# A GCN layer with gated residual and layer norm on one core: the last i-group in three runs of 256, 128 and 128 columns, and another order of the last tiles' small operations

## The chip, the cores and the metric

The program runs on one core of a Trainium2 chip. The metric is device time in microseconds (us). Of the kernel before there are three timed runs, with a median of 396.89 us, and one profiled execution.

## The reference, cut to what matters

There are 4096 nodes with two feature sets of width 128, x and spatial_x, and a dense 4096 x 4096 matrix adj. All is float32.

```python
def _gcn_layer(x, adj, W, b):
    d_inv_sqrt = (jnp.sum(adj, axis=1) + 1e-09) ** (-0.5)
    msg = d_inv_sqrt[:, None] * adj * d_inv_sqrt[None, :] @ x
    return jax.nn.relu(msg @ W + b)
H_f = _gcn_layer(feature_x, adj, W_f, b_f)
H_s = _gcn_layer(spatial_x, adj, W_s, b_s)
attn = jax.nn.sigmoid(jnp.concatenate([H_f, H_s], axis=1) @ W_att + b_att)
x = _layernorm(x + attn * H_f + (1.0 - attn) * H_s, axis=-1)
```

## The kernel before, in words

Nodes are cut into T = 32 tiles of P = 128 and G = 8 i-groups of IB = 512 columns, an i-group being four output tiles (GT). The big product is sums[feature, i] = sum over j of Y[j, feature] * A^T[j, i], where Y is the two feature sets side by side (256 wide), each row scaled by D = degree^-0.5. TensorE does it in blocks (e, t): run e has an i-group, a list of j-tiles t to accumulate over, a PSUM pair and a column range. For each of the two feature halves a block is three matmuls (lines 380 to 382), since each operand is split into a high and a low float32r part: Yh x Ah, Yl x Ah, Yh x Al. Each matmul has its own 128x128 weights (a half of Yh or Yl), and the moving operand is Ah or Al. `plan` lists the runs and groups their blocks into K = 64 items, each one transfer of 1 MB of A^T; ScalarE makes Ah (line 657), VectorE makes Al (line 471). `sweeps(k)` orders an item's blocks: run by run, all tiles of half 0 and then all of half 1. As a run's half ends, VectorE adds it from PSUM to acc (`evacuate_half`, line 493).

In the last 16 items each i-group gets its last eight j-tiles. The last i-group (tiles 28 to 31) is two runs of 256 columns, each one item of eight blocks: tiles 28 and 29, then 30 and 31.

When an i-group is complete, each of its tiles r goes through this chain, over four engines:

- TensorE: product with W_f and W_s (`weigh`, `weigh_half`; line 390, plain float32). `weigh_half` waits for the evacuation of one half, does both tiles, then waits for the other half.
- VectorE: `affine` (line 507, scale and bias into z), `logit` (line 516, max(z,0) times W_att with its sum).
- ScalarE: `relu` (line 688), `gate` (line 693, sigmoid).
- `mix` on GpSimd (lines 803 and 804) or, for the tiles in OWN_MIX, on VectorE (lines 523 and 524): H_f - H_s, and x + H_s.
- VectorE: `join` (line 537), x + H_s + attn * (H_f - H_s) with its row sum.
- GpSimd: `mean` (line 809). ScalarE: `square` (line 697). GpSimd: `deviation` (lines 814, 817 and 822; the power -0.5 and the shift). ScalarE: `normalise` (line 702).
- SP: the store of the tile (line 366), in the order of tiles 0 to 27 and then BY_VECTOR = 30, 28, 29, 31.

The last four tiles differ: VectorE normalises them (`normalise_last`, lines 561 and 565), and tiles 30 and 31 get their statistics on VectorE (`join_last`, lines 546 to 555) and their power on GpSimd (`last_deviation`, line 827). Nothing is scheduled at run time: each engine's order is the order of the code, and inside the item loop `group_at` places a group's steps so many items after its run's end. All that comes after the loop, on each engine, is written out by hand, and that is what the change edits.

Of the kernel before, what the change touches and what calls it, by code (L numbers as in the profile page):

```python
# [24 lines left out]
def plan(T):  # L25
# [43 lines left out]
    order += [(G - 1, s6 + s7), (G, s6 + s7)]  # L69
    items.extend([(first + g, t) for t in s] for g, s in order)  # L70
    return runs, items


def build(nc, At, adj, xs_in, W_f, W_s, b_f, b_s, W_att, b_att, out):
# [11 lines left out]
    FIRST_LAST = len(runs) - G - 1  # L86
# [108 lines left out]
    with ExitStack() as ctx:  # L195
# [175 lines left out]
        def _(pe):  # L371
# [62 lines left out]
            for k in range(K):  # L434
# [25 lines left out]
            weigh_half(HALVES[1])  # L460
# [3 lines left out]
        def _(dve):  # L464
# [76 lines left out]
            def join_last(r):  # L541

                n = r - (T - 2)
# [3 lines left out]
                                         in1=xs[:, r, 0:F], op0=ALU.mult, op1=ALU.add).then_inc(y_ok, 1)  # L547
                dve.wait_ge(y_ok, r + 1)
# [102 lines left out]
        def _(act):  # L651
# [81 lines left out]
            for r in of_group(TAIL - 3):  # L733
                normalise(r)
# [158 lines left out]
```

## Time and profile before

| | us |
|---|---|
| median of 3 runs (396.66 to 397.29) | 396.89 |
| profiled execution, its own time | 398.95 |
| its span, first to last instruction | 397.1 |
| TensorE busy (matmuls) | 373.2 |
| VectorE busy | 296.6 |
| ScalarE busy | 284.6 |
| GpSimd busy | 145.4 |

The profile is of one execution. PE is TensorE's matmuls and PEld its weight loads, DVE is VectorE, ACT is ScalarE, POOL is GpSimd, SP issues the DMAs. Matmuls are pipelined: one of 128x512 is shown as 0.39 us long, but the next starts 0.23 us after it, so what a matmul costs is read from starts, not from lengths.

### The profile page before, as it was taken

The numbers are of one execution on the slowest core, as the hardware profiler recorded it, in microseconds if no ns is written. First come the engines' busy times: TensorE is split into PE (matmuls) and PEld (weight loads), VectorE is DVE, ScalarE is ACT, GpSimd is POOL, SyncE is SP. The second block draws the span as 40 slices with busy tenths as digits, with TensorE's granted clock in tenths as the row PEclk, the third lists the DMA queues.
The fourth block names the chain that finished last, engine by engine and source line by source line (L and its number), as shares of the span: only waits on it lengthen the run. The fifth ranks groups of instructions, "written<-read, shape, count | busy, mean of one in ns | idle before, by whom it ended". The sixth has DMA issues, their size and how long they took to land. (4 is left out here: it accounts for less than half of the span.)

```text
span 397.1 us, 5306 instructions
## 1 busy us (share of the span) xinstructions
PE 373.2 (94%) x1748; PEld 310.7 (78%) x1748; DVE 296.6 (75%) x417; ACT 284.6 (72%) x346; POOL 145.4 (37%) x189
## 2 busy tenths in 40 slices
PE   2997999999999999999999999999889999999991
PEld 2785786878888888888888888888668888888991
DVE  2768984968668793969397775919857797888896
ACT  3777788788878887777878887858492656578565
POOL 1000002571177226730459100002010417877765
PEclk9999999999999999999999999999999999999997
DMA  8999999999999999999999999999946534344011
GB/s 302 415 424 419 419 422 420 420 423 420 422 419 419 420 421 418 363 404 427 421 418 421 416 390 421 414 411 413 360 177 262 210 106 171 149 168 150 19 38 53
DMA packets 25371, 132.86 MB, mean 335 GB/s; under 512 B 2944, under 2 KB 7936, under 8 KB 11008
## 3 DMA queue, kind: packets, MB, share of 16 engines
q1 hardware_dynamic: 25344, 132.53, 82.7%
q8 instruction: 14, 0.23, 0.2%
q14 instruction: 13, 0.11, 0.1%
HBM read 130.42 MB, written 2.10 MB: 334 GB/s over the span
## 5 line engine op out<-in xcount | busy, mean ns | idle before, releaser
L380 PE MATMUL sums<-Ah,Yh 128*128 128x512 f32 (+1 forms) x528 | 204.0, 386 | 7.4 <-DVE Yl L482 4.1
L382 PE MATMUL sums<-Al,Yh 128*128 128x512 f32 (+1 forms) x528 | 202.2, 383 | 0.0
L381 PE MATMUL sums<-Ah,Yl 128*128 128x512 f32 (+1 forms) x528 | 202.2, 383 | 0.0
L471 DVE TENSOR_TENSOR Al<-raw,Ah 128x2048 fp32r<-128x2048 f32 (+1 forms) x70 | 153.6, 2201 | 35.3 <-ACT Ah L657 32.8
L657 ACT ACTIVATE Ah<-raw 128x2048 fp32r<-128x2048 f32 (+1 forms) x70 | 123.2, 1768 | 46.1 <-DMA raw<-in_At 32.3
L670 ACT ACTIVATE nat<-nat 128x2048 f32<-128x2048 f32 x54 | 103.6, 1918 | 28.4 <-DMA nat<-in_adj 27.2
L380 PEld LDWEIGHTS sums<-Ah,Yh 128*128 128x128 f32 x528 | 99.2, 188 | 30.4 <-DVE Yl L482 7.0
L382 PEld LDWEIGHTS sums<-Al,Yh 128*128 128x128 f32 x528 | 99.2, 188 | 19.6
L381 PEld LDWEIGHTS sums<-Ah,Yl 128*128 128x128 f32 x528 | 99.2, 188 | 18.9
L493 DVE TENSOR_TENSOR acc<-sums,acc 128x512 f32<-128x512 f32 (+1 forms) x122 | 77.5, 676 | 45.6 <-PE sums L382 45.6
L797 POOL TENSOR_TENSOR S<-S,raw 128x512 f32<-128x512 f32 x32 | 56.4, 1761 | 24.6 <-DMA raw<-in_At 21.8
L762 POOL TENSOR_SCALAR dg<-rs 128x1 f32<-128x1 f32 x23 | 13.8, 598 | 128.4 <-ACT nat L670 128.2
L697 ACT ACTIVATE fin<-xs,less 128x128 f32<-128x128 f32 x30 | 11.7, 390 | 18.6 <-POOL less L809 18.6
L803 POOL TENSOR_TENSOR fin<-fin 128x128 f32<-128x128 f32 x29 | 13.9, 480 | 21.8 <-ACT fin L688 21.8
L804 POOL TENSOR_TENSOR xs<-xs,fin 128x128 f32<-128x128 f32 x29 | 20.7, 713 | 0.0
L482 DVE SCALAR_TENSOR_TENSOR Yl<-xs,D,Yh 128x256 fp32r<-128x256 f32 x32 | 20.0, 641 | 0.0
L537 DVE SCALAR_TENSOR_TENSOR xs<-fin,att,xs 128x128 f32<-128x128 f32 x30 | 12.3, 423 | 8.6 <-POOL xs L804 8.5
L390 PE MATMUL sums<-Wfs,acc 128*128 128x128 f32 x128 | 16.3, 277 | 0.1
L390 PEld LDWEIGHTS sums<-Wfs,acc 128*128 128x128 f32 x128 | 15.6, 191 | 1.0 <-DVE acc L493 0.3
L681 ACT ACTIVATE Yh<-xs,D 128x256 fp32r<-128x256 f32 x32 | 15.2, 494 | 1.4 <-POOL D L789 0.9
L783 POOL TENSOR_TENSOR dsum<-rs 128x4 f32<-128x4 f32 x2 | 1.9, 975 | 37.8 <-ACT nat L670 19.5
L688 ACT ACTIVATE fin<-nat 128x256 f32<-128x256 f32 x32 | 11.5, 408 | 5.9 <-DVE nat L507 5.8
(49 smaller groups left out, 139.0 us busy)
## 6 DMA issues: line engine op xcount, KB each, us to landing
raw<-in_At SPq DMA_DIRECT2D x64, 1024.0 KB, 9.3
nat<-in_adj SPq DMA_DIRECT2D x48, 1024.0 KB, 11.4
nat<-in_adj SPq DMA_DIRECT2D x8, 768.0 KB, 12.5
xs<-in_xs SPq DMA_DIRECT2D x7, 512.0 KB, 11.3
nat<-in_adj SPq DMA_DIRECT2D x8, 256.0 KB, 9.2
out<-xs SPq DMA_DIRECT2D x32, 64.0 KB, 1.9
xs<-in_xs SPq DMA_DIRECT2D x2, 128.0 KB, 6.8
xs<-in_xs SPq DMA_DIRECT2D x1, 256.0 KB, 11.6
```

What stands on the lines that cost most here:

```text
L380: pe.matmul(to, Yh[:, t % YRING, hs], high, start=first, stop=False)
L381: pe.matmul(to, Yl[:, t % YRING, hs], high, start=False, stop=False)
L382: mm = pe.matmul(to, Yh[:, t % YRING, hs], low, start=False, stop=last)
L390: return pe.matmul(sums[:, 3, bank, c + half * H:c + (half + 1) * H], acc[:, r // GT, half, q * P:(q + 1) * P], Wfs[:, half * H:(half + 1) ...
L471: dve.tensor_tensor(Al[:, k % SPLITS, a * IB:b * IB], raw[:, k % RAWS, a * IB:b * IB], Ah[:, k % SPLITS, a * IB:b * IB], ALU.subtract).the ...
L482: dve.scalar_tensor_tensor(out=Yl[:, r % YRING, :], in0=xs[:, r, :], scalar=D[:, r:r + 1], in1=Yh[:, r % YRING, :].bitcast(F32), op0=ALU.mult,
L493: dve.tensor_tensor(acc[:, g, half, a:b], sums[:, pair, half, 0:b - a], acc[:, g, half, a:b], ALU.add).then_inc(evac_ok, 1)
L657: act.activation(Ah[:, k % SPLITS, a * IB:b * IB], raw[:, k % RAWS, a * IB:b * IB], ACT.Copy).then_inc(high_ok, b - a)
L670: act.activation(nat[:, n % NATS, :], nat[:, n % NATS, :], ACT.Copy, accum_out=rs[:, r, h:h + 1]).then_inc(rs_act, 1)
L681: act.activation(Yh[:, r % YRING, :], xs[:, r, :], ACT.Copy, scale=D[:, r:r + 1]).then_inc(Yh_ok, 1)
L797: pool.tensor_tensor(S[:, g, :], S[:, g, :], raw[:, k % RAWS, j * IB:(j + 1) * IB], ALU.add).then_inc(block_sum_ok, 1)
L804: pool.tensor_tensor(xs[:, r, 0:F], xs[:, r, 0:F], f[:, H_S], ALU.add).then_inc(res_ok, 1)
```

## The change

The second run of the last i-group is cut in two: its 256 columns become one run of 128 columns for tile 30 and one for tile 31, both in the last item, of 16 blocks now. The third run has PSUM pair 1.

```diff
-    runs.append((G - 1, s6 + s7, 2, (0, IB // 2)))
-    runs.append((G - 1, s6 + s7, 0, (IB // 2, IB)))
+    runs.append((G - 1, s6 + s7, 2, (0, 2 * P)))
+    runs.append((G - 1, s6 + s7, 0, (2 * P, 3 * P)))
+    runs.append((G - 1, s6 + s7, 1, (3 * P, IB)))
...
+    items.append([(first + G - 1, t) for t in s6 + s7])
+    items.append([(first + e, t) for e in (G, G + 1) for t in s6 + s7])
...
-    HALVES = [range(LAST, LAST + 2), range(LAST + 2, T)]
-    OWN_MIX = [LAST - 2, LAST - 1, T - 2]
+    LAST_ROWS = [range(LAST, LAST + 2), range(T - 2, T - 1), range(T - 1, T)]
+    PAIR = LAST_ROWS[0]
+    OWN_MIX = [T - 1]
...
-                    if k == K - 1 and step == GT:
-                        weigh_half(HALVES[0])
+                    if k == K - 1 and step == 2 * GT:
+                        weigh_last(0)
+                    if k == K - 1 and step == 6 * GT:
+                        weigh_last(1)
...
-            weigh_half(HALVES[1])
+            weigh_last(2)
```

`weigh_last(n)` is `weigh_half` for the rows of LAST_ROWS[n]: tiles 28 and 29 are weighed after half 0 of the second run, tile 30 after half 0 of the third, tile 31 at the end. On VectorE `join_last` is cut in two: it ends with the join, and `spread_last` does the statistics. The order behind the item loop:

```diff
-            for r in of_group(TAIL - 2):
+            for r, q in zip(of_group(TAIL - 2), of_group(TAIL - 1)):
                 join(r)
+                affine(q)
             evacuate_half(FIRST_LAST + TAIL, 0)
-            for r in of_group(TAIL - 1):
-                affine(r)
             for r in of_group(TAIL - 1):
                 logit(r)
             evacuate_half(FIRST_LAST + TAIL, 1)
-            mix(LAST - 2)
-            mix(LAST - 1)
+            join(LAST - 4)
+            for r in PAIR:
+                affine(r)
+            join(LAST - 3)
             join(LAST - 2)
             join(LAST - 1)
-            join(LAST - 4)
-            for r in HALVES[0]:
-                affine(r)
-            join(LAST - 3)
-            for r in HALVES[0]:
-                logit(r)
             evacuate_half(FIRST_LAST + TAIL + 1, 0)
             evacuate_half(FIRST_LAST + TAIL + 1, 1)
-            for r in HALVES[0]:
-                join(r)
-            for r in HALVES[1]:
-                affine(r)
+            for r in PAIR:
                 logit(r)
-            mix(T - 2)
+            affine(T - 2)
+            logit(T - 2)
+            evacuate_half(FIRST_LAST + TAIL + 2, 0)
+            join(PAIR[0])
+            evacuate_half(FIRST_LAST + TAIL + 2, 1)
+            join(PAIR[1])
             join_last(T - 2)
+            affine(T - 1)
+            logit(T - 1)
+            spread_last(T - 2)
+            mix(T - 1)
             join_last(T - 1)
+            spread_last(T - 1)
```

On ScalarE the relus of group 6 (tiles 24 to 27) come ahead of the squares of group 5, and of group 6 only tile 24 is squared before the gates of tiles 28 to 30; tiles 25 to 27 are squared between gate 30 and relu 31. On GpSimd:

```diff
-            mix(HALVES[0][0])
+            mix(LAST - 4)
+            mean(of_group(TAIL - 2))
+            for r in range(LAST - 3, LAST):
+                mix(r)
+            deviation(of_group(TAIL - 2))
+            mix(PAIR[0])
             mean(of_group(TAIL - 1))
-            mix(HALVES[0][1])
-            mean(HALVES[0])
+            mix(PAIR[1])
+            mix(T - 2)
+            mean(PAIR)
             deviation(of_group(TAIL - 1))
-            mix(T - 1)
             last_deviation([T - 2])
-            deviation(HALVES[0])
+            deviation(PAIR)
             last_deviation([T - 1])
```

What this makes of the engines' orders, at three places.

TensorE in the last item. Before, where tiles 28 and 29 are weighed (L390), amid half 0 of the second run:

```order
L380 MATMUL sums<-Ah,Yh 128x256
L381 MATMUL sums<-Ah,Yl 128x256
L382 MATMUL sums<-Al,Yh 128x256
L390 MATMUL sums<-Wfs,acc 128x128 x4
L380 MATMUL sums<-Ah,Yh 128x256
```

And with the change, where tile 30 is weighed (L393), between the halves of the third run:

```order
L383 MATMUL sums<-Ah,Yh 128x128
L384 MATMUL sums<-Ah,Yl 128x128
L385 MATMUL sums<-Al,Yh 128x128
L393 MATMUL sums<-Wfs,acc 128x128 x2
L383 MATMUL sums<-Ah,Yh 128x128
```

The three lines of a block stand 16 times in the item before, with 256 columns, and 32 times now, with 128.

VectorE from the last two evacuations (L493) on, before; the first two joins (L537) are those of tiles 28 and 29:

```order
L493 TENSOR_TENSOR acc<-sums,acc 128x256 x2
L537 SCALAR_TENSOR_TENSOR xs,ysum<-fin,att,xs 128x128 x2
L507 SCALAR_TENSOR_TENSOR nat<-sums,D,bias 128x256
L516 SCALAR_TENSOR_TENSOR nat,lg<-nat,watt 128x256
L507 SCALAR_TENSOR_TENSOR nat<-sums,D,bias 128x256
L516 SCALAR_TENSOR_TENSOR nat,lg<-nat,watt 128x256
L523 TENSOR_TENSOR fin<-fin 128x128
L524 TENSOR_TENSOR xs<-xs,fin 128x128
L546 SCALAR_TENSOR_TENSOR xs<-fin,att,xs 128x128
L551 BN_STATS st<-xs 128x6
```

With the change, from the affine of tile 30 (L512) on:

```order
L512 SCALAR_TENSOR_TENSOR nat<-sums,D,bias 128x256
L521 SCALAR_TENSOR_TENSOR nat,lg<-nat,watt 128x256
L498 TENSOR_TENSOR acc<-sums,acc 128x128
L542 SCALAR_TENSOR_TENSOR xs,ysum<-fin,att,xs 128x128
L498 TENSOR_TENSOR acc<-sums,acc 128x128
L542 SCALAR_TENSOR_TENSOR xs,ysum<-fin,att,xs 128x128
L549 SCALAR_TENSOR_TENSOR xs<-fin,att,xs 128x128
L512 SCALAR_TENSOR_TENSOR nat<-sums,D,bias 128x256
L521 SCALAR_TENSOR_TENSOR nat,lg<-nat,watt 128x256
L558 BN_STATS st<-xs 128x6
```

The affine and the logit of tile 30 have moved ahead of the last evacuations, and the join of tile 29 (the second L542) still stands behind the very last one.

GpSimd's end before, from the mix of tile 29 on (L803 and L804):

```order
L803 TENSOR_TENSOR fin<-fin 128x128
L804 TENSOR_TENSOR xs<-xs,fin 128x128
L809 TENSOR_TENSOR less<-ysum,share 128x2
L814 TENSOR_SCALAR vare<-ysq 128x4
L817 TENSOR_TENSOR rstd<-vare,mhalf 128x4
L822 TENSOR_TENSOR shift<-less,rstd 128x4
L803 TENSOR_TENSOR fin<-fin 128x128
```

With the change, from the mix of tile 30 on (L812 and L813):

```order
L812 TENSOR_TENSOR fin<-fin 128x128
L813 TENSOR_TENSOR xs<-xs,fin 128x128
L818 TENSOR_TENSOR less<-ysum,share 128x2
L823 TENSOR_SCALAR vare<-ysq 128x4
L826 TENSOR_TENSOR rstd<-vare,mhalf 128x4
L831 TENSOR_TENSOR shift<-less,rstd 128x4
L836 TENSOR_TENSOR rstd<-vare,mhalf 128x1
```

The mean of tiles 28 and 29 stands ahead of the deviation of tiles 24 to 27 in both; the mix of tile 31 no longer follows.

## Rows read from the trace of the kernel before

**Rows 1.** The page, busy time of each engine

```profile
PE 373.2 (94%) x1748; PEld 310.7 (78%) x1748; DVE 296.6 (75%) x417; ACT 284.6 (72%) x346; POOL 145.4 (37%) x189
```

**Rows 2.** Windows: stretch, busy us (instructions) by engine, clock, DMA share, GB/s

```profile
380.10:387.40 7.30, 7.19 (x59) 6.93 (x58) 7.00 (x31) 5.12 (x18) 5.69 (x12) 1.00 0.14 39
```

**Rows 3.** Timeline of PE, 367 to 388 us: start, length, instruction

```profile
367.84 0.39 PE L380 MATMUL sums<-Ah,Yh 128*128 128x512 f32 x1
...
372.60 0.28 PE L380 MATMUL sums<-Ah,Yh 128*128 128x256 f32 x1
...
375.48 1.95 PE L390 MATMUL sums<-Wfs,acc 128*128 128x128 f32 x16
377.18 0.37 PE L380 MATMUL sums<-Ah,Yh 128*128 128x256 f32 x1
...
380.14 0.28 PE L380 MATMUL sums<-Ah,Yh 128*128 128x256 f32 x1
...
381.58 1.43 PE L390 MATMUL sums<-Wfs,acc 128*128 128x128 f32 x8
382.77 0.37 PE L380 MATMUL sums<-Ah,Yh 128*128 128x256 f32 x1
...
387.05 0.28 PE L382 MATMUL sums<-Al,Yh 128*128 128x256 f32 x1
```

**Rows 4.** L424's matmuls by form (busy, mean ns), and timeline of their loads

```profile
L424 PE MATMUL sums<-ones,S 128*128 128x1 f32 x16 | 1.8, 245 | 0.0
252.81 1.88 PEld L424 LDWEIGHTS sums<-ones,S 128*128 128x128 f32 x16
```

**Rows 5.** Timeline of PEld at 37.9 us, after a wait

```profile
37.88 0.19 PEld L380 LDWEIGHTS sums<-Ah,Yh 128*128 128x128 f32 x1 [0.84 <-DVE Yl L482]
37.99 0.19 PEld L381 LDWEIGHTS sums<-Ah,Yl 128*128 128x128 f32 x1
```

**Rows 6.** Timeline of DVE, 387.3 to 389.4 us

```profile
387.37 0.42 DVE L493 TENSOR_TENSOR acc<-sums,acc 128x256 f32<-128x256 f32 x1 [0.30 <-PE sums L382]
...
388.20 0.35 DVE L537 SCALAR_TENSOR_TENSOR xs<-fin,att,xs 128x128 f32<-128x128 f32 x1
...
388.47 0.48 DVE L507 SCALAR_TENSOR_TENSOR nat<-sums,D,bias 128x256 f32<-128x256 f32 x1
388.99 0.42 DVE L516 SCALAR_TENSOR_TENSOR nat<-nat,watt 128x256 f32<-128x256 f32 x1
```

**Rows 7.** Timeline of POOL, 388.7 to 390.8 us

```profile
388.70 0.20 POOL L809 TENSOR_TENSOR less<-ysum,share 128x2 f32<-128x2 f32 x1 [1.09 <-ACT fin L697]
...
390.42 0.33 POOL L822 TENSOR_TENSOR shift<-less,rstd 128x4 f32<-128x4 f32 x1
```

**Rows 8.** Timeline of ACT, 390.5 to 392.9 us

```profile
390.52 0.39 ACT L697 ACTIVATE fin<-xs,less 128x128 f32<-128x128 f32 x1
...
391.30 1.63 ACT L702 ACTIVATE xs<-xs,shift,rstd 128x128 f32<-128x128 f32 x4
```

**Rows 9.** Timeline of the SP queue: the last eight stores

```profile
391.80 3.67 SPq L366 DMA_DIRECT2D out<-xs  x8
```

**Rows 10.** Timeline of all engines, 390 to 394.7 us, tiles 30 and 31

```profile
390.21 0.29 DVE L523 TENSOR_TENSOR fin<-fin 128x128 f32<-128x128 f32 x1
390.41 0.28 DVE L524 TENSOR_TENSOR xs<-xs,fin 128x128 f32<-128x128 f32 x1
...
392.12 0.64 POOL L827 TENSOR_TENSOR rstd<-vare,mhalf 128x1 f32<-128x1 f32 x1 [0.51 <-DVE vare L555]
...
394.34 0.35 DVE L565 TENSOR_SCALAR xs<-xs,mv,rstd 128x128 f32<-128x128 f32 x1
```

**Rows 11.** Timeline of DVE: a join of group 5, and affines 24 to 27

```profile
376.52 0.42 DVE L537 SCALAR_TENSOR_TENSOR xs<-fin,att,xs 128x128 f32<-128x128 f32 x1 [0.45 <-POOL xs L804]
...
378.88 1.65 DVE L507 SCALAR_TENSOR_TENSOR nat<-sums,D,bias 128x256 f32<-128x256 f32 x4
```

**Rows 12.** Timeline of POOL: the mix of tile 20

```profile
374.62 0.46 POOL L803 TENSOR_TENSOR fin<-fin 128x128 f32<-128x128 f32 x1
375.04 0.46 POOL L804 TENSOR_TENSOR xs<-xs,fin 128x128 f32<-128x128 f32 x1
```

More of the change, by code:

```diff
@@ L65, in plan @@
     runs.extend((g, s6 + s7, (g + 1) % 3, (0, IB)) for g in range(G - 1))
-    runs.append((G - 1, s6 + s7, 2, (0, IB // 2)))
-    runs.append((G - 1, s6 + s7, 0, (IB // 2, IB)))
+    runs.append((G - 1, s6 + s7, 2, (0, 2 * P)))
+    runs.append((G - 1, s6 + s7, 0, (2 * P, 3 * P)))
+    runs.append((G - 1, s6 + s7, 1, (3 * P, IB)))
     order = [(0, s6), (1, s6), (0, s7), (1, s7)] + [(g, s) for g in range(2, G - 1) for s in (s6, s7)]
-    order += [(G - 1, s6 + s7), (G, s6 + s7)]
     items.extend([(first + g, t) for t in s] for g, s in order)
+    items.append([(first + G - 1, t) for t in s6 + s7])
+    items.append([(first + e, t) for e in (G, G + 1) for t in s6 + s7])
     return runs, items
@@ L85, in build @@
     FINAL = K - 2 * G
-    FIRST_LAST = len(runs) - G - 1
+    FIRST_LAST = len(runs) - (G - 1) - 3
     BLK = GT * IB
@@ L175, in build @@
     LAST = (G - 1) * GT
-    HALVES = [range(LAST, LAST + 2), range(LAST + 2, T)]
-    OWN_MIX = [LAST - 2, LAST - 1, T - 2]
-    BY_VECTOR = [T - 2, *HALVES[0], T - 1]
+    LAST_ROWS = [range(LAST, LAST + 2), range(T - 2, T - 1), range(T - 1, T)]
+    PAIR = LAST_ROWS[0]
+    OWN_MIX = [T - 1]
+    BY_VECTOR = [T - 2, *PAIR, T - 1]
     POOL_MIX = [r for r in range(T) if r not in OWN_MIX]
@@ L402, in weigh, with weigh_last @@
                     weigh_tile(r, 1).then_inc(w_ok, 1)
-            def weigh_half(rows):
-                part = HALVES.index(rows)
-                evacuated = 2 * evac_no[FIRST_LAST + TAIL + part]
+            def weigh_last(n):
+                rows = LAST_ROWS[n]
+                evacuated = 2 * evac_no[FIRST_LAST + TAIL + n]
                 pe.wait_ge(z_ok, rows[0])
@@ L541, in join_last @@
             def join_last(r):
-                n = r - (T - 2)
                 dve.wait_ge(gate_ok, r + 1)
@@ L547, in join_last, with spread_last @@
                                          in1=xs[:, r, 0:F], op0=ALU.mult, op1=ALU.add).then_inc(y_ok, 1)
+            def spread_last(r):
+                n = r - (T - 2)
                 dve.wait_ge(y_ok, r + 1)
@@ L557, in normalise_last @@
             def normalise_last(r):
-                if r in HALVES[0]:
-                    dve.wait_ge(rstd_ok, HALVES[0][-1] + 1)
-                    dve.wait_ge(less_ok, HALVES[0][-1] + 1)
+                if r in PAIR:
+                    dve.wait_ge(rstd_ok, PAIR[-1] + 1)
+                    dve.wait_ge(less_ok, PAIR[-1] + 1)
                     dve.tensor_scalar(xs[:, r, 0:F], xs[:, r, 0:F], less[:, r:r + 1], rstd[:, r:r + 1],
@@ L734, in _ @@
                 normalise(r)
+            for r in of_group(TAIL - 1):
+                relu(r)
             for r in of_group(TAIL - 2):
                 square(r)
-            for r in of_group(TAIL - 1):
+            gate(of_group(TAIL - 1))
+            for r in PAIR:
                 relu(r)
-            gate(of_group(TAIL - 1))
             for r in of_group(TAIL - 2):
                 normalise(r)
-            for r in HALVES[0]:
-                relu(r)
             square(LAST - 4)
-            square(LAST - 3)
-            gate(HALVES[0])
-            square(LAST - 2)
-            square(LAST - 1)
-            for r in HALVES[1]:
-                relu(r)
-                gate([r])
-            for r in HALVES[0]:
+            gate(PAIR)
+            relu(T - 2)
+            gate([T - 2])
+            for r in of_group(TAIL - 1)[1:]:
+                square(r)
+            relu(T - 1)
+            gate([T - 1])
+            for r in PAIR:
                 square(r)
@@ L848, in of_group @@
                 return range(g * GT, (g + 1) * GT)
-            for g in range(TAIL):
+            for g in range(TAIL - 1):
                 if g >= 1:
@@ L854, in _ @@
                 for r in of_group(g):
-                    if r not in OWN_MIX:
-                        mix(r)
-            mix(HALVES[0][0])
+                    mix(r)
+            mix(LAST - 4)
+            mean(of_group(TAIL - 2))
+            for r in range(LAST - 3, LAST):
+                mix(r)
+            deviation(of_group(TAIL - 2))
+            mix(PAIR[0])
             mean(of_group(TAIL - 1))
-            mix(HALVES[0][1])
-            mean(HALVES[0])
+            mix(PAIR[1])
+            mix(T - 2)
+            mean(PAIR)
             deviation(of_group(TAIL - 1))
-            mix(T - 1)
             last_deviation([T - 2])
-            deviation(HALVES[0])
+            deviation(PAIR)
             last_deviation([T - 1])
```

## The prediction

> **What bounds the kernel now.** I read the page first: TensorE is busy 94% of the span [rows 1], so the kernel is TensorE's stream of matmuls, and what follows its last product. Its granted clock in the stretch of the last item is 1.00, the 2.4 GHz level [rows 2]. Then I read the timelines of the last 25 us, because the diff touches nothing before 372 us. TensorE's rows show no gap: the first run of the last i-group starts at 372.60, the second at 380.14, and its last accumulating matmul starts at 387.05 and takes 0.28, so sums are complete at 387.33; only one short wait lies in between, before 382.77 [rows 3]. The chain behind that is this. VectorE adds the last half at 387.37, makes joins 28 and 29 (end 388.55) [rows 6]; GpSimd has `mean(28, 29)` and `deviation(24..27)` queued behind join 29, from 388.70 to 390.75 [rows 7]; ScalarE squares tiles 28 and 29 and then normalises 24 to 27 from 391.30, four in 1.63 us and 0.39 apart, so the first ends at 391.77 [rows 8]; the SP queue issues the last eight stores one after another from 391.80 to 395.47 [rows 9], and the span closes at 397.1. Tile 31's own end (norm at 394.34 to 394.69) comes before its place in that queue. So the page's chain, which ends in that last norm, is about 0.4 us short of being the bound: the stores are a queue of eight times 0.46 us, started by the normalisation of tile 24. From the last sum to the first of these stores it is 391.80 - 387.33 = 4.47 us, and 5.3 more to the end of the span.
>
> **What one matmul of 128 columns costs.** This is the term that decides, and no accumulating matmul of that width runs now. In a stream, 24 matmuls of 256 columns take 372.60 to 375.48, 120 ns each; 21 of 512 columns take 367.84 to 372.60, 227 ns each [rows 3]. The 256 more columns cost 107 ns, so columns cost 0.417 ns, and 13 ns are fixed. By that line 128 columns take 53 + 13 = 67 ns. But each matmul here loads its own weights. The 16 passes of L424 multiply only one column each, and still their 16 loads take 1.88 us, the last alone 0.19, so fifteen steps of 112 ns [rows 4]: nothing is left there but the load of 128x128 four-byte weights. That those are plain f32 and ours float32r makes no difference where I can see it: after a stall, when the next load is free to go, L381's load follows L380's by 0.11 us (37.88, 37.99) [rows 5]. A load hides behind 256 columns (107 + 13 > 112), not behind 128. So I take 112 ns; the ends from the nearest rows are 67 ns below (the line through the two widths), 108 ns for the closest reading of the loads, and 120 ns above (the 256-column matmul; half of it can't cost more unless the hardware treats narrow ones in another way, a rival below).
> The Trainium skill (TensorE: Matmul & The Clock Gate, section Back-to-back issue gap) speaks for the change: it gives about 81 ns per matmul of 128 columns in streams of load and matmul, and 56 ns without the load. By 81 ns the time would be 398.1 us as an estimate, by 56 ns 395.7. No row here shows a pitch under 108 ns, and the one-column passes contradict both for four-byte weights.
>
> **The change, part by part.**
> *Last i-group in three runs.* Removed are the 48 matmuls of 256 columns of the second run (48 x 120 ns = 5.8 us), added 96 of 128 columns (96 x 112 ns = 10.75 us). The products with W_f and W_s after 380.14 stay 12 passes until the last sum of the third run starts (8 for tiles 28 and 29, now 4 for tile 30 too; before it was 8): 12 x 112 ns = 1.35 us. Before, the wait at 381.58 to 382.77 held 0.3 us for the evacuation of the first run's second half; it goes, since that is done by 381.7 and now asked for at 382.8. The last sum is complete at 380.14 + 10.75 + 1.35 + 0.17 (the last matmul takes 0.28, not 0.11) = **392.41**, against 387.33: +5.08 us.
> *What follows the last sum.* VectorE adds the last 128 columns (256 take 0.42; with half the columns I let the next operation start after 0.23), then join 29 with 0.35 [rows 6]: 392.45 to 393.03. GpSimd again has `mean(28, 29)` and `deviation(24..27)` queued behind it, the wait that matters: 388.55 to 390.75 is 2.20 us [rows 6, 7], now 393.03 to 395.23. ScalarE has to pass gate 31 and the squares of 28 and 29 first. TensorE's last product needs the evacuation (392.7) and ends about 393.2; affine 31 goes behind joins 29 and 30, 393.4 to 393.9, logit 31 to 394.4 (0.48 and 0.42, 0.52 from the one to the other [rows 6]), gate 31 at 394.45, the squares behind it from 394.65 with 0.39 each [rows 8], so ScalarE is free at 395.43. The normalisation of tile 24 takes 0.48: first store at **395.94**, 3.53 us behind the last sum where it was 4.47. Before, four vector operations for tile 30 and the affine of 31 stood between join 29 and ScalarE's squares; now tile 30 has been sent ahead.
> *Stores.* SP's instructions are unchanged: eight at the same pace, so the end moves with the first, 395.94 - 391.80 = **+4.14 us**. Tile 31 does not take over: from gate 31 at 394.75 with the mix (two of 0.29, 0.20 apart), join, statistics and a power of 0.64 [rows 10] its norm ends near 398.2, about 3.4 us on, and its slot in the queue is at 399.2.
> *Affines laced into joins.* Four joins of group 5 each wait some 0.45 us for a mix on GpSimd [rows 11]; the affines of 24 to 27 (0.39 apart in their stream) now fill those waits, so VectorE is about 1 us earlier at logit 27. That is taken at nothing: VectorE then waits for TensorE, at the next affine already (381.8 to 383.7) and again at 386.6 and 389.7. If TensorE were not late, this 1 us would be the gain.
> *Mixes.* Mixes 26, 27 and 30 go from VectorE (0.40 each) to GpSimd (0.42 for each of two operations [rows 12]), mix 31 the other way. GpSimd idles from about 387.1 to 390.7 in my schedule, waiting for tile 30, so it costs nothing; mix 31 on VectorE stands in the tail of tile 31, covered by the 1.0 us that tile 31 has in hand.
> *Squares, deviations, runs' places in PSUM and the load of the last item* move behind work that is already waiting; that item is as many bytes as before, and the bank of the third run was emptied at 375. Nothing.
>
> **Sum.** +4.1 us. The profiled execution took 398.95 us around its span of 397.1; with the change 403.1. The median of the runs shown, 396.89, is 0.5% under that execution, and the same step on it gives **401.0 us**. With 108 ns a matmul it is 0.4 less, with 120 ns 0.8 more; the tail worked out may be 0.6 off either way: 399.6 to 402.6 for this case.
>
> **Rivals.**
> *The load hides after all.* Float32r weights could be loaded behind the running matmul as long as it streams, so that only 67 ns are left. Then the last sum is complete at 380.14 + 6.43 + 1.35 + 0.22 = 388.14, and with 3.53 us the first store is at 391.67: -0.1 us, 396.8, not slower; it decides from a pitch of 68 ns down, below which the change wins, up to 0.9 us with the scatter of the tail. For it: the fixed 13 ns at both widths show no load at all. Against it: [rows 4, 5].
> *A narrow float32r matmul is run as a plain f32 one.* L390's f32 products of 128 columns appear as two passes each, 16 rows for 8 instructions, 1.70 us from 375.48 to the next matmul at 377.18 and so 106 ns a pass [rows 3], 112 by [rows 4]. If that held for the 96, each would take up to 223 ns: 21.4 us in place of 10.75, so 411.6. For it: only that width and this price stand side by side in the trace. Against it: float32r at 256 and 512 columns is a single pass, and nothing in the instruction but its width changes.
> *The change does what it says and the shorter tail wins.* The tail is 0.94 us shorter in my working; for a gain, TensorE would have to lose less than that, which is the first rival's condition and no case of its own.
>
> **Chances.** 112 ns and its bounds 0.80; hidden loads 0.12; two passes 0.08. Around 396.8, with its scatter, the hidden-load case is 0.04 faster by over 0.2%, 0.05 within 0.2% (0.8 us, about what a measurement can tell here), and 0.03 slower. So faster 0.04, same 0.05, slower 0.91. The predicted time is the likeliest case's. Its own range holds about 0.77; I reach down to 397.6, the slower part of the hidden-load case, and leave the two-pass case out: 397.6 to 402.6.
>
> **What would show it.** Right: matmul rows of 128x128 in the last item 0.11 us apart and their weight loads back to back; the last of them near 392.3; GpSimd's mean of two tiles near 393.2; the first of the last eight stores near 395.9; VectorE with waits of 1 to 2 us for TensorE. Wrong: such rows 0.07 or 0.22 apart, or first store and last sum more than 4.5 or less than 2.5 us apart.

## The result, and the profile after

The changed kernel takes 400.65 us (median of 4 runs, 400.58 to 401.14), the kernel before 397.07 in the runs made beside it: ratio 1.0094, 95% interval 1.0076 to 1.0111. It is slower by 3.6 us. Its profiled execution took 400.63 us around a span of 398.8.

The page of the changed kernel, busy time of each engine, which answers to [rows 1]; its matmuls of 128 columns by form (busy, mean ns | idle before); and a windows row of the narrow stretch with the columns of [rows 2]:

```profile
PE 378.9 (95%) x1796; PEld 316.9 (79%) x1796; DVE 296.3 (74%) x415; ACT 284.6 (71%) x346; POOL 152.7 (38%) x193
```

```profile
L383 PE MATMUL sums<-Ah,Yh 128*128 128x128 f32 x32 | 8.8, 275 | 0.0
```

```profile
377.95:390.30 12.35, 12.35 (x113) 12.34 (x111) 7.70 (x32) 6.65 (x26) 6.93 (x15) 1.00 0.08 23
```

48 more matmuls, TensorE without a gap and its loads busy for 12.34 of 12.35 us, at the 2.4 GHz level. VectorE, busy for 7.00 of 7.30 us in the last stretch before [rows 2], now idles 38% of it. The timeline of PE answers to [rows 3]:

```profile
370.50 0.28 PE L383 MATMUL sums<-Ah,Yh 128*128 128x256 f32 x1
...
378.04 0.22 PE L383 MATMUL sums<-Ah,Yh 128*128 128x128 f32 x1
378.10 0.28 PE L384 MATMUL sums<-Ah,Yl 128*128 128x128 f32 x1
378.21 0.27 PE L385 MATMUL sums<-Al,Yh 128*128 128x128 f32 x1
...
379.44 0.27 PE L384 MATMUL sums<-Ah,Yl 128*128 128x128 f32 x1
...
386.92 0.66 PE L393 MATMUL sums<-Wfs,acc 128*128 128x128 f32 x4
387.34 0.31 PE L383 MATMUL sums<-Ah,Yh 128*128 128x128 f32 x1
...
389.94 0.28 PE L385 MATMUL sums<-Al,Yh 128*128 128x128 f32 x1
390.05 1.03 PE L393 MATMUL sums<-Wfs,acc 128*128 128x128 f32 x4
```

From 378.10 to 379.44 are twelve steps: 112 ns each. The last sum is complete at 389.94 + 0.28 = 390.22 (390.21 unrounded).

The clocks of the two executions can't be compared directly. In this one the first matmul of 256 columns starts at 370.50, in the one before at 372.60 [rows 3], with the same code ahead of it; in the executions below it lies anywhere from 370.4 to 372.5, and in one, two_runs_both, at 377.2. What the stretch after it takes repeats much better. So from here on each kernel is counted from its own first matmul of 256 columns (in four_runs, the first of 128):

| us | before | changed |
|---|---|---|
| first such matmul to the last sum | 14.73 | 19.71 |
| last sum to the first of the last eight stores | 4.47 | 3.37 |
| that store to the end of the span | 5.27 | 5.26 |
| together | 24.47 | 28.34 |

That is +3.87 us, against +3.6 in the medians. The tail behind the last sum, in timelines of DVE, POOL, ACT and SP ([rows 6 to 9]):

```profile
390.25 0.29 DVE L498 TENSOR_TENSOR acc<-sums,acc 128x128 f32<-128x128 f32 x1 [1.00 <-PE sums L385]
390.46 0.34 DVE L542 SCALAR_TENSOR_TENSOR xs<-fin,att,xs 128x128 f32<-128x128 f32 x1
```

```profile
390.95 0.19 POOL L818 TENSOR_TENSOR less<-ysum,share 128x2 f32<-128x2 f32 x1 [1.40 <-DVE xs L542]
...
392.60 0.35 POOL L831 TENSOR_TENSOR shift<-less,rstd 128x4 f32<-128x4 f32 x1
```

```profile
392.69 0.39 ACT L706 ACTIVATE fin<-xs,less 128x128 f32<-128x128 f32 x1
...
393.08 1.63 ACT L711 ACTIVATE xs<-xs,shift,rstd 128x128 f32<-128x128 f32 x4
```

```profile
383.32 13.91 SPq L369 DMA_DIRECT2D out<-xs  x12
```

The chain is the forecast one: join 29, GpSimd's mean and deviation behind it, ScalarE's squares, the normalisation of tile 24, and a queue of eight stores (393.58 to 396.81; the profile prints them with the four of group 5). Where VectorE's time went is in its waits (the number before the arrow): 1.00 us above, and 2.13 us before affine 30:

```profile
387.62 0.48 DVE L512 SCALAR_TENSOR_TENSOR nat<-sums,D,bias 128x256 f32<-128x256 f32 x1 [2.13 <-PE sums L393]
```

### The profile page after: what moved, and what is told of

Its sections match the earlier page's. It is cut to its first block and busy times, and to the rows that moved or that the text cites. A ratio compares the mean times of both kernels' runs of the same rounds, so it can differ in the third digit from the quotient of the medians.

```text
span 398.8 us, 5407 instructions
## 1 busy us (share of the span) xinstructions
PE 378.9 (95%) x1796; PEld 316.9 (79%) x1796; DVE 296.3 (74%) x415; ACT 284.6 (71%) x346; POOL 152.7 (38%) x193
## 5 line engine op out<-in xcount | busy, mean ns | idle before, releaser
L383 PE MATMUL sums<-Ah,Yh 128*128 128x512 f32 (+2 forms) x544 | 208.8, 384 | 3.9 <-DVE Yl L487 2.2
L384 PE MATMUL sums<-Ah,Yl 128*128 128x512 f32 (+2 forms) x544 | 207.1, 381 | 0.0
L385 PE MATMUL sums<-Al,Yh 128*128 128x512 f32 (+2 forms) x544 | 206.9, 380 | 0.0
L383 PEld LDWEIGHTS sums<-Ah,Yh 128*128 128x128 f32 x544 | 102.7, 189 | 26.1 <-DVE Yl L487 4.6
L385 PEld LDWEIGHTS sums<-Al,Yh 128*128 128x128 f32 x544 | 102.8, 189 | 19.7
L384 PEld LDWEIGHTS sums<-Ah,Yl 128*128 128x128 f32 x544 | 102.8, 189 | 19.1
L498 DVE TENSOR_TENSOR acc<-sums,acc 128x512 f32<-128x512 f32 (+2 forms) x124 | 77.7, 665 | 45.7 <-PE sums L385 45.7
L771 POOL TENSOR_SCALAR dg<-rs 128x1 f32<-128x1 f32 x23 | 20.2, 880 | 121.2 <-ACT nat L679 121.0
L806 POOL TENSOR_TENSOR S<-S,raw 128x512 f32<-128x512 f32 x32 | 55.3, 1729 | 23.8 <-DMA raw<-in_At 21.0
L812 POOL TENSOR_TENSOR fin<-fin 128x128 f32<-128x128 f32 x31 | 15.2, 491 | 25.6 <-ACT fin L697 25.6
L813 POOL TENSOR_TENSOR xs<-xs,fin 128x128 f32<-128x128 f32 x31 | 21.7, 699 | 0.0
L542 DVE SCALAR_TENSOR_TENSOR xs<-fin,att,xs 128x128 f32<-128x128 f32 x30 | 12.7, 436 | 7.2 <-POOL xs L813 7.1
L393 PE MATMUL sums<-Wfs,acc 128*128 128x128 f32 x128 | 16.3, 277 | 0.1
L512 DVE SCALAR_TENSOR_TENSOR nat<-sums,D,bias 128x256 f32<-128x256 f32 x32 | 13.7, 477 | 3.6 <-PE sums L393 3.5
L393 PEld LDWEIGHTS sums<-Wfs,acc 128*128 128x128 f32 x128 | 15.6, 191 | 0.8 <-DVE acc L498 0.3
```

The costliest lines, as they stand in the source:

```text
L383: pe.matmul(to, Yh[:, t % YRING, hs], high, start=first, stop=False)
L384: pe.matmul(to, Yl[:, t % YRING, hs], high, start=False, stop=False)
L385: mm = pe.matmul(to, Yh[:, t % YRING, hs], low, start=False, stop=last)
L393: return pe.matmul(sums[:, 3, bank, c + half * H:c + (half + 1) * H], acc[:, r // GT, half, q * P:(q + 1) * P], Wfs[:, half * H:(half + 1) ...
L498: dve.tensor_tensor(acc[:, g, half, a:b], sums[:, pair, half, 0:b - a], acc[:, g, half, a:b], ALU.add).then_inc(evac_ok, 1)
L771: pool.tensor_scalar(dg[:, r:r + 1], rs[:, r, 0:1], rs[:, r, 1:2], 1e-9, ALU.add, ALU.add).then_inc(dg_ok, 1)
```

## The experiments

**Is it the split alone?** old_split is the changed kernel with the last i-group in two runs of 256 columns again and everything else as changed.

```diff
-    runs.append((G - 1, s6 + s7, 0, (2 * P, 3 * P)))
-    runs.append((G - 1, s6 + s7, 1, (3 * P, IB)))
+    runs.append((G - 1, s6 + s7, 0, (2 * P, IB)))
...
-    LAST_ROWS = [range(LAST, LAST + 2), range(T - 2, T - 1), range(T - 1, T)]
+    LAST_ROWS = [range(LAST, LAST + 2), range(T - 2, T)]
-    OWN_MIX = [T - 1]
+    OWN_MIX = [T - 2]
```

> The last i-group is again two runs of 256 columns with TensorE's order of the kernel before; the new order of the small operations stays as far as it doesn't hang on the third run (affines laced into joins, mixes 26 and 27 on GpSimd, all squares before relu 30; tile 30 mixed on VectorE and tile 31 on GpSimd as before). My theory (112 ns for each of the 96 narrow matmuls is the whole loss, the order costs nothing): 396.5 us, 0.6 under the kernel before, since VectorE no longer holds back TensorE's wait of 0.3 us in the last item and its tail starts that much earlier; last sum 14.4 us after the first matmul of 256 columns, before it was 14.7. Rival (the new order of small operations is a good part of the 3.6 us, for instance the mixes moved to GpSimd): 398 to 399.5 us with the last sum where it was.

397.3 us, ratio 1.0003 (0.9995 to 1.0012): 14.79 to the last sum, 4.37, 5.27, together 24.43 where before has 24.47. The whole loss is the split's. The laced affines and the other orders, worth nothing in the changed kernel, are worth nothing here either, where I had expected 0.6 us from them. The fifth experiment shows why.

**What sets the 112 ns?** Two kernels change the narrow matmuls alone: narrow_64 gives each only 64 of its 128 columns, two_products leaves out the product with Yl in them, a third of the matmuls.

```diff
-                to = sums[:, pair, half, 0:b - a]
+                w = 64 if b - a == P else b - a
+                to = sums[:, pair, half, 0:w]
...
-                cols = slice(j * (b - a), (j + 1) * (b - a))
+                cols = slice(j * (b - a), j * (b - a) + w)
```

> As the changed kernel, but the matmuls of its second and third run take only the first 64 of their 128 columns, so half the columns of tiles 30, 31 are left out of the big product. If the load of the weights sets the pace (my theory), the 96 rows stay 112 ns apart and the time stays 400.65 within 0.2%. If columns set it (a fixed part and 0.417 ns a column, or two passes of 128 columns), the pace falls by 27 ns or more: 96 x 27 ns = 2.6 us less, 398.1.

```diff
-                pe.matmul(to, Yl[:, t % YRING, hs], high, start=False, stop=False)
-                mm = pe.matmul(to, Yh[:, t % YRING, hs], low, start=False, stop=last)
+                if b - a == P:
+                    mm = pe.matmul(to, Yh[:, t % YRING, hs], low, start=False, stop=last)
+                else:
+                    pe.matmul(to, Yl[:, t % YRING, hs], high, start=False, stop=False)
+                    mm = pe.matmul(to, Yh[:, t % YRING, hs], low, start=False, stop=last)
```

> As the changed kernel, but for the second and third run the product of Yl with Ah is left out, so 64 narrow matmuls in place of 96. If the end follows TensorE one to one: 32 x 112 ns = 3.6 us less, 397.1, about the time of the kernel before, with the first of the last eight stores as much earlier. If the stores, GpSimd or VectorE set the end behind the last sum by themselves, less comes through: 398.5 or more.

two_products took 397.42 us, ratio 1.0013 (1.0004 to 1.0022), and 16.25 us to the last sum: 32 matmuls fewer are 3.46 us less, 108 ns each. It has the changed kernel's tail (3.37), so it also shows what that tail is worth: a last sum 1.5 us later than before costs only 0.13%. As an estimate from these rows, the split would pay if it cost TensorE less than some 1.1 us (4.47 - 3.37).

narrow_64 took 405.2 us, ratio 1.019 (1.0167 to 1.0213), slower still, which neither theory had. Windows of its last stretch:

```profile
372.50:380.00 7.50, 7.50 (x65) 7.48 (x64) 6.34 (x24) 4.97 (x14) 6.77 (x16) 1.00 0.13 36
380.00:387.70 7.70, 7.70 (x70) 7.70 (x69) 6.02 (x25) 4.55 (x18) 5.95 (x13) 0.97 0.11 31
387.70:396.50 8.80, 8.80 (x43) 8.80 (x42) 1.59 (x6) 2.05 (x9) 0.92 (x2) 0.50 0.02 5
```

While the clock holds the theory is right: half the columns, and the pitch (the time from one start to the next) is still 112 ns. So columns don't set it. What is left is what each narrow matmul brings with it whatever its width, one load of 128x128 weights, and two loads behind one another are 0.11 us apart even where the matmuls are wide ([rows 5]). That a smaller load, or none, would be cheaper is not shown: every matmul of every run has a full one. Then, at 387.29, about 1 us into the last run and with TensorE busy without a gap since 380, the granted clock falls to 0.50, the 1.2 GHz level, and the pitch becomes 213 ns. The last sum is 24.04 us out instead of 19.71.

**Is a longer stretch of 128 columns safe from that?** four_runs cuts the first half of the last i-group in two as well, so all 192 of its matmuls have 128 columns.

```diff
-    runs.append((G - 1, s6 + s7, 2, (0, 2 * P)))
-    runs.append((G - 1, s6 + s7, 0, (2 * P, 3 * P)))
-    runs.append((G - 1, s6 + s7, 1, (3 * P, IB)))
+    runs.append((G - 1, s6 + s7, 2, (0, P)))
+    runs.append((G - 1, s6 + s7, 0, (P, 2 * P)))
+    runs.append((G - 1, s6 + s7, 1, (2 * P, 3 * P)))
+    runs.append((G - 1, s6 + s7, 2, (3 * P, IB)))
```

> As the changed kernel, but its first run of 256 columns is cut in two of 128 as well, so 192 narrow matmuls in place of 96 and 48 wide ones. Only loads count, clock stays (theory): 48 x 120 ns = 5.8 us go, 96 x 112 ns = 10.75 us come, +5.0 us, 405.6 us; first narrow matmul to last sum 24.7 us. Rival, since the run with 64 columns showed it: TensorE's granted clock falls to its 1.2 GHz level within the longer stretch of narrow matmuls though no matmul waits; then rows come 213 ns apart from there on and the time is 410 us or more.

406.4 us, ratio 1.0238 (1.0194 to 1.0283), and 24.68 us from the first narrow matmul to the last sum, where 24.7 was expected. TensorE's loss doubles with the number of narrow matmuls, from 4.98 to 9.95 us (24.68 - 14.73); the time, forecast at 405.6, grows by somewhat more than twice 3.6, since the shorter tail is gained only once. The clock holds throughout (windows):

```profile
371.80:396.40 24.60, 24.60 (x222) 24.57 (x221) 13.79 (x56) 11.63 (x40) 13.65 (x30) 1.00 0.08 23
```

narrow_96 looks between the two widths: as narrow_64, with 96 in the place of 64.

> The changed kernel with 96 of the 128 columns in each matmul of the second and third run (a quarter of the columns of tiles 30 and 31 is left out of the big product). If a narrow matmul costs its weight load, the pitch stays at 0.112 us and the time at 400.6, as long as the granted clock stays at the 2.4 GHz level. In narrow_64 the clock fell to 1.2 GHz 7.3 us after the first narrow matmul, with no idle time before it, and in four_runs (128 columns) it held for 24.7 us. [...]

405.06 us, ratio 1.0195 (1.018 to 1.0209), and 24.08 us to the last sum. I had put it at 22 to 24 us and 403 to 405 if the clock fell here too, and at 19.7 and 400.6 if it held: it falls. Windows, and the timeline of PE at the fall:

```profile
377.90:385.40 7.50, 7.50 (x69) 7.50 (x68) 6.05 (x25) 4.46 (x17) 5.99 (x13) 0.98 0.10 30
385.40:394.40 9.00, 9.00 (x44) 9.00 (x43) 1.59 (x6) 2.16 (x9) 0.91 (x2) 0.50 0.02 7
```

```profile
384.92 0.28 PE L385 MATMUL sums<-Ah,Yl 128*128 128x96 f32 x1
385.03 0.29 PE L386 MATMUL sums<-Al,Yh 128*128 128x96 f32 x1
385.14 0.39 PE L384 MATMUL sums<-Ah,Yh 128*128 128x96 f32 x1
385.33 0.41 PE L385 MATMUL sums<-Ah,Yl 128*128 128x96 f32 x1
385.55 0.41 PE L386 MATMUL sums<-Al,Yh 128*128 128x96 f32 x1
```

The clock falls at 385.16, and the steps grow from 0.11 to 0.21 us there. It is no chance of one execution: the mean granted clock of the four timed runs is 0.978 to 0.983 in narrow_64 and 0.977 to 0.980 in narrow_96, and 0.992 to 0.995 in the changed kernel. The same number of instructions, 0.11 us apart and with no idle time before the fall, and one width keeps the clock where two smaller ones lose it. What the chip goes by, these runs don't show; it stays open.

**Are the stores the bound behind the last sum?** two_queues lets ScalarE issue the stores of tiles 24 to 27 behind its normalisations, and leaves the others on SP; before_two_queues is the same edit in the kernel before.

```diff
-            for r in [*range(LAST), *BY_VECTOR]:
+            for r in [*range(LAST - GT), *BY_VECTOR]:
...
+            for r in of_group(TAIL - 1):
+                act.wait_ge(norm_ok, r + 1)
+                act.dma_start(out_v[r], xs[:, r, 0:F]).then_inc(stored, 16)
```

> As the changed kernel, but the stores of tiles 24 to 27 are issued on ScalarE's own queue behind its normalisations, the other four by SP as before. If the queue of eight stores ends last (my theory): the end is that of tile 31's normalisation and one store, span 1.2 us shorter, 399.5 us or a little under. If the normalisation of tile 31 ends last (what the page's chain says): no change, 400.65; and an issue on ScalarE that is slower than SP's would show as longer.

> The kernel before, but with the stores of tiles 24 to 27 on ScalarE's queue. By my reading of the kernel before the queue of eight ends 0.35 us behind what tile 31's normalisation allows: 396.7 us against 397.05. If the last normalisation is the bound already: 397.05.

two_queues took 400.28 us (ratio 1.0083, 1.0069 to 1.0097), 27.51 us from the first matmul of 256 columns to the end, 0.83 less than the changed kernel, where 1.2 was expected; the medians, 0.4 apart and with overlapping intervals, show less. before_two_queues took 397.23 (0.9999, 0.9979 to 1.0019), together 24.47: nothing, where 0.35 was expected. The queues of before_two_queues (issuing spans and counts), and VectorE's normalisations of tiles 28, 29 and 31:

```profile
393.19 2.09 SPq L366 DMA_DIRECT2D out<-xs  x4
```

```profile
393.62 0.60 DVE L561 TENSOR_SCALAR xs<-xs,less,rstd 128x128 f32<-128x128 f32 x2 [0.46 <-POOL rstd L820]
394.14 0.35 DVE L565 TENSOR_SCALAR xs<-xs,mv,rstd 128x128 f32<-128x128 f32 x1
```

Half the queue is gone, but its second half had no slack: tile 28 is normalised only from 393.62, and the three stores behind it still go out 0.4 to 0.5 us apart. The end is two bounds lying on each other, the queue and VectorE's normalisations, and taking away one is worth what the other leaves.

**Did the laced affines do anything?** no_lacing puts the affines of 24 to 27 behind the four joins and the evacuation again, in the changed kernel.

```diff
-            for r, q in zip(of_group(TAIL - 2), of_group(TAIL - 1)):
+            for r in of_group(TAIL - 2):
                 join(r)
-                affine(q)
             evacuate_half(FIRST_LAST + TAIL, 0)
+            for r in of_group(TAIL - 1):
+                affine(r)
```

> As the changed kernel, but the affines of tiles 24 to 27 come behind the four joins and one evacuation again, as in the kernel before. VectorE waits 1 to 2 us for TensorE three times behind it, so by my reading nothing changes: 400.65 within 0.2%. If the lacing is worth anything in this kernel, 401.5 or more.

400.76 us, ratio 1.008 (1.0054 to 1.0107), 19.71 us to the last sum and 28.34 in all: unchanged, as expected. With the split, VectorE waits for TensorE anyway, ahead of affine 30 for 2.13 us with the lacing and for 1.63 without it.

But in old_split that wait is not there. The timelines of DVE of the kernel before and of the changed one show what became of the saving; the logits of tiles 24 to 27, the first and the last of before, the first three of the changed kernel:

```profile
380.45 0.42 DVE L516 SCALAR_TENSOR_TENSOR nat<-nat,watt 128x256 f32<-128x256 f32 x1
...
381.48 0.42 DVE L516 SCALAR_TENSOR_TENSOR nat<-nat,watt 128x256 f32<-128x256 f32 x1
```

```profile
377.66 0.41 DVE L521 SCALAR_TENSOR_TENSOR nat<-nat,watt 128x256 f32<-128x256 f32 x1
...
378.00 0.67 DVE L521 SCALAR_TENSOR_TENSOR nat<-nat,watt 128x256 f32<-128x256 f32 x1
...
378.60 0.67 DVE L521 SCALAR_TENSOR_TENSOR nat<-nat,watt 128x256 f32<-128x256 f32 x1
```

and POOL of the changed kernel beside them:

```profile
378.35 0.64 POOL L812 TENSOR_TENSOR fin<-fin 128x128 f32<-128x128 f32 x1
378.95 0.64 POOL L813 TENSOR_TENSOR xs<-xs,fin 128x128 f32<-128x128 f32 x1
```

The first logit starts 7.85 us after the first matmul of 256 columns before, and 7.16 in the changed kernel: the lacing saved 0.7 us. The last logit makes way for the evacuation at 381.82 - 372.60 = 9.22 and at 379.80 - 370.50 = 9.30: all of it is gone. While GpSimd mixes, a logit takes 0.60 us in place of 0.34, and a mix operation 0.60 in place of 0.42; they start in turns. The Trainium skill (SBUF — State Buffer, section Who interferes with whom) says that a VectorE instruction with two SBUF inputs contends with a GpSimd one that reads SBUF; the logit has two such inputs. The evacuation, with one input in PSUM, keeps its 0.41. The same section of the Trainium skill calls what the two engines share an exclusive lock. By that the pair would take 0.34 + 0.42 = 0.76 us, as an estimate; the trace has 0.60, so here they overlap in part. The kernel before has such rows too, where GpSimd mixes beside the logit of tile 28:

```profile
385.45 0.68 DVE L516 SCALAR_TENSOR_TENSOR nat<-nat,watt 128x256 f32<-128x256 f32 x1
```

```profile
385.81 0.64 POOL L804 TENSOR_TENSOR xs<-xs,fin 128x128 f32<-128x128 f32 x1
```

So this price could have been read ahead of the change.

old_split_own_mixes tries it: old_split with mixes 26 and 27 back on VectorE, behind the joins of 24 and 25.

```diff
-    OWN_MIX = [T - 2]
+    OWN_MIX = [LAST - 2, LAST - 1, T - 2]
...
+            mix(LAST - 2)
+            mix(LAST - 1)
             join(LAST - 2)
             join(LAST - 1)
...
-            for r in range(LAST - 3, LAST):
-                mix(r)
+            mix(LAST - 3)
```

> old_split with the mixes of tiles 26 and 27 given back to VectorE, so that GpSimd has less to do beside the logits of group 6. Theory (VectorE's logits of 128x256 take 0.67 us in place of 0.42 because GpSimd reads and writes beside them): two of the four logits are at 0.42 to 0.45 again, GpSimd's own operations beside none of them are at 0.46, and VectorE pays 4 x 0.29 to 0.40 us for the two mixes where it has time; the evacuation of the first run's second half comes up to 0.5 us earlier, TensorE's wait of 0.18 us for it goes or shrinks, and the time is 397.0 to 397.3, no difference to old_split that 3 rounds would show. Rival (the logits are slow from something else, the wider operand or TensorE's stream): all four stay at 0.67.

396.47 us, ratio 0.9989 (0.9979 to 0.9999), 14.36 to the last sum, together 23.99: better than the 397.0 to 397.3 that I expected, and by its interval barely faster than the kernel before. DVE of it, and then the products of tiles 28 and 29 on PE, in old_split first:

```profile
378.00 0.67 DVE L518 SCALAR_TENSOR_TENSOR nat<-nat,watt 128x256 f32<-128x256 f32 x1
...
378.61 0.41 DVE L518 SCALAR_TENSOR_TENSOR nat<-nat,watt 128x256 f32<-128x256 f32 x1
...
378.95 0.42 DVE L518 SCALAR_TENSOR_TENSOR nat<-nat,watt 128x256 f32<-128x256 f32 x1
```

```profile
380.06 0.61 PE L392 MATMUL sums<-Wfs,acc 128*128 128x128 f32 x4
380.85 0.71 PE L392 MATMUL sums<-Wfs,acc 128*128 128x128 f32 x4 [0.18 <-DVE acc L495]
381.32 0.37 PE L382 MATMUL sums<-Ah,Yh 128*128 128x256 f32 x1
```

```profile
379.49 1.06 PE L392 MATMUL sums<-Wfs,acc 128*128 128x128 f32 x8
380.30 0.37 PE L382 MATMUL sums<-Ah,Yh 128*128 128x256 f32 x1
```

One logit still has a mix beside it and takes 0.67; the next two have none and take 0.41 and 0.42. The evacuation comes at 8.79 us, TensorE does not wait, and its eight passes with the next matmul take 0.81 us in place of 1.26: the wait printed as 0.18 cost 0.45. The printed wait counts only from the end of the fourth pass as it is shown, 380.67, and in a stream the fifth starts long before that. By starts it came 0.79 us behind the first, where half of 0.81 is 0.40.

**A version that beats both?** two_runs_reordered is old_split with joins 28 and 29 ahead of the last half's evacuation, and tiles 28 and 29 ahead of tile 30 in the deviations, normalisations and stores. On ScalarE (not shown) the gate of 28 and 29 comes ahead of the last normalisation of group 5, and their squares ahead of relu 30.

```diff
-    BY_VECTOR = [T - 2, *PAIR, T - 1]
+    BY_VECTOR = [*PAIR, T - 2, T - 1]
...
-            evacuate_half(FIRST_LAST + TAIL + 1, 1)
             for r in PAIR:
                 join(r)
+            evacuate_half(FIRST_LAST + TAIL + 1, 1)
...
             deviation(of_group(TAIL - 1))
+            deviation(PAIR)
```

> Two runs of 256 columns with another order than either kernel: joins 28 and 29 ahead of the last evacuation, the gate of 28 and 29 behind three of the normalisations of group 5, all squares ahead of relu 30, deviations of 24 to 27 and of 28, 29 ahead of the mix of tile 31, stores in order of tile. The power of tile 31 then no longer queues behind the deviation of 28 and 29 (0.5 us), and the stores begin 0.7 us earlier: 396.4 us, 0.6 under the kernel before. Rival: what TensorE's last product lets through (affine 30 starts 1.05 us behind the last sum) and VectorE's row of tile 30 and 31 set the end, 397.0.

397.01 us, ratio 0.9997 (0.9969 to 1.0026): the rival's number. The first store comes 3.62 us behind the last sum (4.37 in old_split), but the eight take 3.80 us in place of 3.24, for VectorE normalises 28, 29, 30 and 31 only at the end: together 24.27. So the next kernel gives 28 and 29 to ScalarE.

```diff
-    BY_VECTOR = [*PAIR, T - 2, T - 1]
+    BY_VECTOR = [T - 2, T - 1]
...
-            for r in of_group(TAIL - 1):
+            for r in [*of_group(TAIL - 1), *PAIR]:
                 normalise(r)
```

> In two_runs_reordered the last eight stores leave in 3.8 us, and the last ones are tiles that VectorE normalises one after the other. Here tiles 28 and 29 get their shift on GpSimd and are normalised on ScalarE behind 24 to 27 (0.39 us each), so VectorE has only 30 and 31 left, and the stores leave in the order of the tiles. Theory (the end is set by VectorE's own work for tile 31 and not by the queue): VectorE loses two normalisations of about 0.4 us ahead of it, the span behind the first matmul of 256 columns is some 0.45 us shorter than in two_runs_reordered (24.27), so about 23.8, and the time is 396.4 to 396.6. Rival (the queue of eight stores at 0.4 to 0.47 us each sets the end, started by the normalisation of tile 24): the same 24.3 us and 397.0.

396.65 us beside 397.17 for the kernel before, ratio **0.9982 (0.9972 to 0.9992)**; 14.84, 3.63 and 5.26, together 23.73, where 23.8 was forecast. It is the only version with an interval clearly under 1, though its median and that of old_split_own_mixes (396.47, taken beside it) can't be told apart. Its SP queue, and VectorE's end:

```profile
388.94 3.67 SPq L368 DMA_DIRECT2D out<-xs  x8
```

```profile
391.10 0.34 DVE L564 TENSOR_SCALAR xs<-xs,mv,rstd 128x128 f32<-128x128 f32 x1
391.90 0.34 DVE L564 TENSOR_SCALAR xs<-xs,mv,rstd 128x128 f32<-128x128 f32 x1 [0.45 <-POOL rstd L822]
```

Tile 31 is normalised at 391.90 + 0.34 = 392.24, and its store, the last, goes out 0.03 us later: now VectorE's last normalisation sets the end.

two_runs_both adds the edit of old_split_own_mixes to it.

> two_runs_pair_on_act with the mixes of tiles 26 and 27 on VectorE again, so both edits that were worth something, in one kernel. Theory (the two are independent: the one takes TensorE's wait for the evacuation away, ahead of the last sum, the other shortens what follows it): first matmul of 256 columns to the last sum 14.4 us (14.84 there), from it to the end of the span 23.3 us (23.73 there, 23.99 in old_split_own_mixes), and the time 396.0 to 396.3, faster than the kernel before by 0.2 to 0.3%. Rival (the tail takes it back: GpSimd's deviation of group 6 or ScalarE's squares are late for their own reasons, and the norm of tile 24 does not come earlier with the last sum): last sum at 14.4, end still 23.7 and 396.65.

396.85 us, ratio 0.9985 (0.996 to 1.001). In its profiled execution (403.15 us) the granted clock was at 0.50 for 3.4 us from 299.2 on, in a wait of TensorE of 3.75 us for VectorE's Yl (printed before its matmul at 299.56) and behind it, long ahead of the stretch. So only what happens from 377.20 on is read; there it is 1.00 up to the last sum. The last sum is at 14.36, as in theory, but the first store comes 4.04 us behind it in place of 3.63, and the end 24.16 after the start: the rival, and 0.4 us more than it had (23.7). ScalarE's gate of 28 and 29, behind which it squares tiles 24 to 27, in two_runs_pair_on_act and then in two_runs_both:

```profile
384.08 0.30 ACT L691 ACTIVATE att<-lg,batt 128x2 f32<-128x2 f32 x1 [0.48 <-DVE nat L518]
```

```profile
391.16 0.30 ACT L693 ACTIVATE att<-lg,batt 128x2 f32<-128x2 f32 x1 [1.63 <-DVE nat L518]
```

13.61 us after the first matmul of 256 columns in the one, 13.96 in the other: the two mixes on VectorE (four operations, 1.35 us) hold up the logits of 28 and 29, and ScalarE waits 1.63 us for them. Behind its squares GpSimd's deviations and then its mix of tile 31 come late, and join 31 waits for that mix:

```profile
397.25 0.35 DVE L546 SCALAR_TENSOR_TENSOR xs<-fin,att,xs 128x128 f32<-128x128 f32 x1 [0.53 <-POOL xs L803]
```

What TensorE wins, VectorE loses. One execution shows this; the times of both kernels are the same within the intervals.

## Why the prediction was right

- **Sign, size and range.** 401.0 forecast with 397.6 to 402.6, 400.65 measured; slower was given 0.91.
- **A matmul of 128 columns, 112 ns.** Measured 112 ns over twelve steps. narrow_64 and narrow_96 show the same pitch with fewer columns as long as the clock holds, and two_products shows that the time goes by the number of matmuls. A narrow matmul costs what its load costs; the rivals of 67 and 223 ns are out. That no row shows a pitch under 108 ns was loosely said, since the prediction itself reads 106 ns for the 16 passes of L390; but the matmul behind them takes 0.20 us (377.18 to 377.38) in place of 0.12, and seventeen steps from 375.48 to 377.38 are 112 ns each. The Trainium skill's 81 ns for such streams (TensorE: Matmul & The Clock Gate, section Back-to-back issue gap) is not what four-byte weights do here.
- **Last sum.** 19.81 us after the first matmul of 256 columns by the working (392.41 - 372.60), 19.71 measured. From the first narrow matmul, 7.54 us after that start in both, it was 12.27 and is 12.17.
- **The wait of 0.3 us goes.** It does. What it was worth had been put a little low: the eight passes around it take 382.77 - 381.58 = 1.19 us, and 0.81 without a wait in old_split_own_mixes, so 0.38 and not 0.3.
- **The tail.** 3.53 forecast for last sum to first store, 3.37 measured: GpSimd's deviation ends 2.74 us behind the last sum (2.82 forecast), ScalarE is free at 2.87 (3.02). The eight stores take what they took.
- **Tile 31.** Its norm ends at 395.51, 5.30 us behind the last sum where 5.8 was forecast, with 1.3 us in hand before its store at 396.81. With the queue shortened, in two_queues, the end moves by only 0.83 of these 1.3 us; the stores of tiles 30, 28 and 29 still stand ahead of tile 31's.
- **The stores as the one bound: too simple.** The prediction has the end of the kernel before set by the queue of eight. before_two_queues gains nothing by halving it, since tiles 28 and 29 are normalised too late for the second half. The forecast did not suffer, because from the first start to the last the eight stores take 3.24 us before and 3.23 now.
- **The sum.** +4.14 forecast, +3.87 measured in the stretch, +3.6 in the medians. The other 0.3 us I put down to the scatter of what lies ahead, which is not shown. The range was a little wider than its own terms, which give 400.0 to 402.4.
- **Laced affines at nothing: right, by the reason given.** The sentence behind it, that VectorE is about 1 us earlier at logit 27 and this would be the gain if TensorE were not late, is wrong: it is 0.7 us earlier at logit 24 and no earlier behind logit 27.
- **Mixes on GpSimd "cost nothing": wrong, and covered.** I asked only whether GpSimd had time. The step that failed is that it takes VectorE's time as well, 0.26 us of each logit. In the changed kernel TensorE's lateness covers that, which is luck and not the reason given; in old_split it is why 397.3 was measured and not 396.5.

## What to carry to other kernels

Before cutting a matmul into narrower ones, ask whether its weights are loaded anew each time: where they are, count loads, and find their price in the trace from the narrowest matmul there is (here passes of one column, 112 ns). In this kernel, cutting below the width that hides the load, some 240 columns as an estimate from 13 + 0.417 ns a column, buys an earlier start of what follows at the full price of the load; it pays only if what follows gains more. And when work moves from VectorE to an idle GpSimd, look at what VectorE runs meanwhile.

## What the runs showed of the hardware that was not expected

- **The granted clock fell in a stream without a gap.** TensorE's rows are busy throughout and the matmuls 0.11 us apart, yet with 64 and with 96 columns each the clock went from 1.00 to 0.50 about 1 us into the last run (at 387.29 and 385.16), and the pitch from 112 to 213 ns. With 128 columns it stayed at 1.00 for the whole 24.6 us. So here a matmul that costs only its load was not safe to make narrower than 128 columns.
- **A matmul that costs its load follows the same clock:** 213 ns at 1.2 GHz against 112 at 2.4.
- **VectorE and GpSimd slow each other:** logit 0.34 to 0.60 us, mix operation 0.42 to 0.60, start to start, in the changed kernel, and the logits return to 0.34 where the mix is taken away.
- **A store costs its issuer about the same on either queue:** ScalarE's four start 0.42 to 0.49 us apart in two_queues, SP's eight 0.38 to 0.47 in the changed kernel.
